# Attention groups in pairs on TensorE, turned context and 8-bit q, k, v

## The reference

```
def _fq(x, delta, zp, n_bits):
    xi = round(x / delta) + zp
    return (clip(xi, 0, 2**n_bits - 1) - zp) * delta
def _attn(x, ctx, wq, wk, wv, wo, bo, dq, dk, dv, dw):
    q, k, v = heads(x @ wq), heads(ctx @ wk), heads(ctx @ wv)      # 16 heads of 32
    sim  = _fq(q, dq, 128, 8) @ _fq(k, dk, 128, 8).T * SCALE
    attn = softmax(sim)
    out  = _fq(attn, dw, 0, 8) @ _fq(v, dv, 128, 8)
    return out @ wo + bo
h1 = _ln(x, ln1_g, ln1_b)
x = _attn(h1, h1, a1_wq, a1_wk, a1_wv, a1_wo, a1_bo, ...) + x
h2 = _ln(x, ln2_g, ln2_b)
x = _attn(h2, context, a2_wq, a2_wk, a2_wv, a2_wo, a2_bo, ...) + x
# then: layer norm, gated feed forward, residual; then block L1
```

## Time and profile before

| | us |
|---|---|
| median of 3 runs (2874.74 to 2876.45) | 2874.8 |
| the profiled execution | 2874.01 |
| its span, first to last instruction | 2872.2 |
| TensorE busy | 2700.3 (94%) |
| VectorE busy | 1690.5 (59%) |
| ScalarE busy | 1454.0 (51%) |
| GpSimd busy | 688.8 (24%) |

### The profile page before, as it was taken

The page is one execution under the profiler, slowest core; times in us unless marked ns, Lnnn a source line. Parts: engine busy times, 40 slices in busy tenths (PEclk is TensorE's granted clock), DMA queues, the critical chain, the costliest instruction groups (busy, mean ns, idle before and its releaser), DMA issues.

```text
span 2872.2 us, 54738 instructions
## 1 busy us (share of the span) xinstructions
PE 2700.3 (94%) x18432; PEld 2199.8 (77%) x18432; DVE 1690.5 (59%) x4154; ACT 1454.0 (51%) x3765; POOL 688.8 (24%) x1147
## 2 busy tenths in 40 slices
PE   5799999999999997589999999999999999999997
PEld 4566666666666665289999999999888888888885
DVE  6788888888888886453434343435434434434433
ACT  5577777777777775321111111113455555555554
POOL 1222222222222221132323232322212212212211
PEclk9899999999999998699999999999999999999998
DMA  5343333434334432441111111124111111111111
GB/s 151 85 85 83 83 82 84 84 83 88 84 80 86 91 77 59 107 135 66 66 66 66 67 64 73 58 80 155 38 44 48 55 44 44 58 44 44 58 37 37
DMA packets 337322, 211.07 MB, mean 73 GB/s; under 512 B 275568, under 2 KB 291952, under 8 KB 337264
## 3 DMA queue, kind: packets, MB, share of 16 engines
q1 hardware_dynamic: 337264, 210.34, 27.1%
HBM read 92.84 MB, written 50.33 MB: 50 GB/s over the span
## 4 chain that ended last, share of the span: by engine, by line
PE 54%; DVE 2%; issue 1%; ACT 1%; DMA 0%; POOL 0%; DVEq 0%; SPq 0%; POOLq 0%
PE AG L158 33%; PE Y L158 12%; PE XT L1287 2%; PE O L1310 2%; PE XT L1297 2%; PE XT L133 1%; DVE parts L1631 1%; DVE xhat L125 1%; PE Y L133 0%; PE O L1320 0%; DVE turned L187 0%; ACT stage L1527 0%; DMA stage<-in_ff_w_dram 0%; DVE mid_parts L1688 0%; POOL base L1841 0%
## 5 line engine op out<-in xcount | busy, mean ns | idle before, releaser
L158 PE MATMUL AG<-h_parts,up 128*128 128x256 f32 x6144 | 778.9, 285 | 13.4 <-DVE down L1612 10.1
L158 PEld LDWEIGHTS AG<-h_parts,up 128*128 128x128 f32 x6144 | 762.9, 193 | 25.9 <-issue 10.9
L594 ACT ACTIVATE e<-S,bias,qk_scale 128x256 f32<-128x256 f32 x1024 | 563.1, 563 | 66.7 <-DVE pq L707 62.9
L1495 ACT ACTIVATE gate<-AG,cols_pack 128x256 f32<-128x256 f32 x256 | 121.5, 474 | 671.3 <-PE AG L158 670.8
L1856 POOL TENSOR_TENSOR mid_parts<-mid_act,mid_parts 128x256 fp32r<-128x256 f32 x256 | 199.6, 780 | 1078.3 <-DVE mid_parts L1688 1078.3
L689 DVE TENSOR_REDUCE negmax<-S 128x4 f32<-128x1024 f32 x256 | 312.3, 1220 | 170.2 <-PE S L502 169.5
L158 PE MATMUL Y<-down,mid_parts 128*128 128x512 f32 x1536 | 403.8, 400 | 0.0
L1681 DVE SCALAR_TENSOR_TENSOR mid_act<-AG,cols_pack,gate 128x256 f32<-128x256 f32 x256 | 123.3, 482 | 423.9 <-ACT gate L1495 423.0
L158 PEld LDWEIGHTS Y<-down,mid_parts 128*128 128x128 f32 x1536 | 272.1, 189 | 68.5 <-issue 22.6
L707 DVE TENSOR_SCALAR pq<-e,rsum 128x256 uint16<-128x256 f32 x1024 | 291.9, 348 | 5.0
L564 ACT ACTIVATE shifted<-PJ,round_col,inv 128x512 f32<-128x512 f32 x192 | 149.2, 777 | 209.6 <-PE PJ L158 208.7
(11 more groups left out here) (131 smaller groups left out, 3707.0 us busy)
## 6 DMA issues: line engine op xcount, KB each, us to landing
stage<-in_ff_w_dram SPq DMA_DIRECT2D x48, 256.0 KB, 4.6
x_in<-in_x_dram SPq DMA_DIRECT2D x16, 512.0 KB, 3.7
ctx_in<-in_ctx_dram SPq DMA_DIRECT2D x16, 512.0 KB, 3.7
mid_dram<-x SPq DMA_DIRECT2D x16, 512.0 KB, 2.8
own<-mid_dram SPq DMA_DIRECT2D x16, 512.0 KB, 3.3
own<-in_ctx_dram SPq DMA_DIRECT2D x16, 512.0 KB, 3.5
h_dram<-h3T SPq DMA_DIRECT2D x16, 512.0 KB, 2.7
k_dram<-own SPq DMA_DIRECT2D x16, 512.0 KB, 2.6
```

Source lines behind the costliest of these rows:

```text
L158: last = nc.tensor.matmul(acc, lhs(l), rhs(r), start=(start and i == 0), stop=(stop and i == 2))
L594: nc.scalar.activation(e[:, s, i, :], S[s][:, i // 2, i % 2, :], ACT.Exp, bias=bias[:, s, i:i + 1], scale=qk_scale[:, ph.a:ph.a + 1], accu ...
L1495: nc.scalar.activation(gate[:, f % 2, :], AG[f % 2][:, TOK:2 * TOK], ACT.Gelu, bias=ff_b1[:, c:c + 1]).then_inc(gate_done, 1)
```

## The change

- Groups run through TensorE in pairs. At each odd g the scores of groups g + 1 and g + 2 are computed together: for each query tile four heads, one behind the other, on rows 0, 32, 64, 96, in four banks. They use both S tiles and wait for the exponentials of all groups up to g. Behind them come the products of the pair g - 5, g - 4, again four heads side by side for each half of the keys. pT has 4 buffers for 2.
- ctx arrives from the host in a turned layout; its transposes and the copies out of PSUM go, the casts and subtractions of high and low parts stay and are placed by group (`ctx_at`).
- ScalarE writes q, k, v as 8-bit integers (scaled copy, rounding and clipping in the conversion); VectorE only widens them to 16 bits, two groups after the fill where the clip was one group after.
- The order on the engines: ScalarE quantises and turns after a group's exponentials instead of before; VectorE computes quotients first and then, at odd g, both maxima; oT is copied at groups 0 and 4 of the next phase. k2's second fill moves ahead of q2, h2T from group 0 to 1, statistics of x from group 3 to 4.

The diff, cut to its core:

```diff
-                        4: [("ctxT", 0), ("ctxT", 1), ("o1", 0)], 5: [("o1", 1)], 6: [("v1", 0)], 7: [("v1", 1)]}
-        PHASE1_FILLS = {0: [("h2T", 0), ("h2T", 1), ("k2", 0)], 1: [("q2", 0)], 2: [("q2", 1)], 3: [("k2", 1)],
+                        4: [("o1", 0)], 5: [("o1", 1)], 6: [("v1", 0)], 7: [("v1", 1)]}
+        PHASE1_FILLS = {0: [("k2", 0)], 1: [("h2T", 0), ("h2T", 1), ("k2", 1)], 2: [("q2", 0)], 3: [("q2", 1)],
...
+            q8 = sb(one, "q8", [P, 2, D], I8)
+            pT = sb(one, "pT", [P, PAIR_BUFS, 4 * TT, P], F16)
...
             def pe_scores(pe, ph, g):
-                    pe.wait_ge(exp_done, 4 * (ph.group(g) - 1))
+                    pe.wait_ge(exp_done, 4 * ph.group(g))
+                for qt in range(TT):
+                    for i in range(4):
+                        r = DH0 * i
+                        ins = nc.tensor.matmul(S[i // 2][:, i % 2, qt, :],
+                                               qT[ph.tiles][r:r + DH0, g // 2, qt * P:(qt + 1) * P],
+                                               kT[ph.tiles][r:r + DH0, g // 2, :], start=True, stop=True)
...
             def pe_pv(pe, ph, g):
+                for kc in range(TT):
+                    for i in range(4):
+                        h = 2 * g + i
+                        r = DH0 * i
+                        c = 4 * (i % 2) + kc
                         ins = nc.tensor.matmul(O[half][r:r + DH0, (h // 4) % 2, :],
                                                vQ[ph.tiles][:, kc, h * DH0:(h + 1) * DH0],
+                                               pT[:, (g + i // 2) % PAIR_BUFS, c:c + 3:2, :], start=(kc == 0),
...
             def pe_phase(pe, ph, prev, nxt):
                 for g in range(GROUPS):
+                    if g % 2:
+                        if g + 1 < GROUPS:
+                            pe_scores(pe, ph, g + 1)
+                        elif nxt:
+                            pe_scores(pe, nxt, 0)
+                        if g >= 5:
+                            pe_pv(pe, ph, g - 5)
+                        elif prev:
+                            pe_pv(pe, prev, g + GROUPS - 5)
+                    for name, j in ph.steps(g):
+                        pe_fill(pe, at(ph.stage, ph.b, name, j))
...
-                nc.scalar.activation(shifted[:, bank, :], PJ[bank][:], ACT.Identity, bias=round_col[:, 0:1],
+                nc.scalar.activation(q8[:, bank, :], PJ[bank][:], ACT.Copy,
                                      scale=inv[:, d:d + 1]).then_inc(pj_emptied[bank], 1)
...
             def act_phase(act, ph, prev):
+                    if prev and g in (0, 4):
+                        act_oT(act, prev, g // 4)
+                    act_exp(act, ph, g)
+                    for where in late(ph, prev, g):
+                        if kind_of(where[2]) in QUANTISED:
+                            act_quantise(act, where)
+                    for where in transposed(ph, g, 0):
+                        act_transposed(act, where)
+                    if g == ph.ctx_at:
+                        act_ctx_high(act, ph, prev)
...
+            def dve_widen(dve, where):
+                wait_emptied(dve, where)
+                nc.vector.tensor_copy(dst, q8[:, bank, :]).then_inc(quantised, 1)
...
             def dve_phase(dve, ph, prev, nxt):
+                    fills = [f for f in late(ph, prev, g, 2) if kind_of(f[2]) in QUANTISED]
+                    if g:
+                        dve_probs(dve, ph, g - 1, fills)
+                    elif prev:
+                        dve_probs(dve, prev, GROUPS - 1, fills)
+                    into, m = (ph, g + 1) if g + 1 < GROUPS else (nxt, 0)
+                    if g % 2 and into:
+                        dve_max(dve, into, m)
+                    for where in transposed(ph, g, 1):
+                        dve_transposed(dve, where)
+                    if g % 2 and into:
+                        dve_max(dve, into, m + 1)
+                    if g == ph.ctx_at:
+                        dve_ctx(dve, ph, prev)
...
             def pool_phase(pool, ph, nxt):
+                    if g % 2:
+                        pool_dsum(pool, ph, g)
                      if g + 1 < GROUPS:
                         pool_bias(pool, ph, g + 1)
...
-                    pool_dsum(pool, ph, g)
+                    if g % 2 == 0:
+                        pool_dsum(pool, ph, g)
...
-                        sp.dma_start_transpose(pT[:, g % 2], pq[:, g % 2].rearrange("p j n -> p (j n)")).then_inc(
+                        sp.dma_start_transpose(pT[:, g % PAIR_BUFS],
...
-                        sp.dma_start(ctx_in[:], ctx_v[seq]).then_inc(ctx_loaded, 16)
+                        sp.dma_start(ctx_in[:], t["ctxT"][seq]).then_inc(ctx_loaded, 16)
```

More of the change, by code:

```diff
@@ L229, in build @@
         ROUNDS = B - 3
+        PAIR_BUFS = 4
         def bank_of(stage, name, j):
-            return 1 - j if name == "q2" else j
+            return 1 - j if name == "q2" and stage == "last" else j
         def fills_of(stage, bank):
@@ L272, in __init__ @@
                 self.tiles = a if tiles is None else tiles
+                self.ctx_at = {id(PHASE2_FILLS): 4, id(P_A_FILLS): 4, id(P_Y_FILLS): 0}.get(id(fills))
+                self.ctx_seq = 0 if stage == "first" else b + 1
                 self.early = ("o1", 1) in fills.get(3, [])
@@ L305, in turned_before @@
                 n += len(those("peeled"))
[L306 to L309, removed]
+            return n + len(those(stage, ORDER[stage][:ORDER[stage].index((name, j))]))
         WEIGHTS = ("a1_wq", "a1_wk", "a1_wv", "a2_wk", "a2_wq", "a2_wv")
@@ L342, in build @@
             x_in = sb(one, "x_in", [P, TT, D])
-            ctx_in = sb(one, "ctx_in", [P, TT, D])
+            ctx_in = sb(one, "ctx_in", [P, KC, TOK])
             x_bo = sb(one, "x_bo", [P, TT, D])
@@ L462, in pe_fill @@
                     ins = transpose_chunks(PJ[bank], xhat, j)
-                elif kind == "ctxT":
-                    seq = 0 if stage == "first" else b + 1
-                    pe.wait_ge(ctx_loaded, 16 * (seq + 1))
-                    ins = transpose_chunks(PJ[bank], ctx_in, j)
                 elif kind in ("o1", "o2"):
@@ L483, in pe_fill @@
                     from_ctx = kind in ("k2", "v2")
-                    pe.wait_ge(turned_low_done, 2 * turned_before(*where, ("ctxT",) if from_ctx else ("hT", "h2T")))
+                    if from_ctx:
+                        pe.wait_ge(ctx_low_done, 2 * (1 if stage == "first" else b + 2))
+                    else:
+                        pe.wait_ge(turned_low_done, 2 * turned_before(*where))
                     w = "a" + kind[1] + "_w" + kind[0]
@@ L604, in act_oT, with late @@
                                      scale=wv_scale[:, ph.a:ph.a + 1]).then_inc(oT_done, 1)
-            def late(ph, prev, g):
-                p, s = (ph, g - 1) if g else (prev, GROUPS - 1)
+            def late(ph, prev, g, by=1):
+                p, s = (ph, g - by) if g >= by else (prev, g + GROUPS - by)
                 if p is None:
                     return []
-                return [at(p.stage, p.b, n, j) for n, j in p.steps(s) if kind_of(n) not in ("hT", "h2T", "ctxT")]
+                return [at(p.stage, p.b, n, j) for n, j in p.steps(s) if kind_of(n) not in ("hT", "h2T")]
             def transposed(ph, g, j):
                 return [at(ph.stage, ph.b, n, i) for n, i in ph.steps(g)
-                        if kind_of(n) in ("hT", "h2T", "ctxT") and i == j]
+                        if kind_of(n) in ("hT", "h2T") and i == j]
             def act_phase(act, ph, prev):
@@ L708, in dve_probs @@
                                             ALU.mult, ALU.min).then_inc(prob_scaled, 1)
-                for where in fills:
-                    dve_unshift(dve, where)
             def dve_residual(dve, where):
@@ L779, in dve_drain @@
                 dve_probs(dve, ph, GROUPS - 1)
-                for where in late(None, ph, 0):
-                    dve_quantise(dve, where)
             def pool_bias(pool, ph, g):
```

224 lines of the change are left out of this document (83 added, 141 removed).

## The result

The changed kernel takes 2835.2 us (median; 2833.2 to 2836.7), the one before 2874.8 on the same chip: ratio 0.986, interval 0.984 to 0.987. It is faster by 39.6 us, less than half of the 87 forecast. The profiled execution has a span of 2834.9 us (before 2872.2). Its page: busy time by engine, and the granted clock of TensorE in 40 slices, in tenths.

A forecast was written before the change was run, and what follows sets the result against it. TensorE's own work was taken to bound the loop, then a chain a pair. 13 rounds from 68.5 to 64.0 us give -58.5, with the ends -87.3: 2788 us forecast, range 2762 to 2850.

The forecast's parts named there:

- Part 4: Cost of pairing in the attention loop: a chain closes once a pair; eight cycles between score bursts sum to 62.9 us.
- cycle 2/7: Phase 2, pair started by odd group 7 (v1, k2): 7.8 us, xhat between max and quotients delaying the second group.
- The clock term: Loop: one drop of TensorE's clock allowed a round, 1.1 us after the spare 0.4, making the round 64.0.
- Cycle 1/5: Phase 1, pair started by odd group 5 (o2, v2): 7.6 us between score bursts, with residual and xhat.
- 2/1: Phase 2, pair started by odd group 1 (q1, k1): 6.9 us between score bursts, set by the exponentials' chain.
- 2/3: Phase 2, pair started by odd group 3 (k1, o1): 7.5 us, the cast of ctx adding 0.55 on ScalarE.
- 1/3: Phase 1, pair started by odd group 3 (q2, o2): 7.1 us between score bursts, set by TensorE.
- second rival: Loop: dearer hand-overs, two or three clock drops a round or widening at 0.69; round 65.5 to 67.5, 2807 to 2835; chance 0.20.
- Part 1: Scores and products, four heads side by side: eight matmuls in 0.22 us where two groups took 0.65, saving 6.9 a round.
- Parts 2 and 3: Turned ctx saves 1.2 us of TensorE; 8-bit q, k, v: ScalarE's pass 0.6, conversion 0.34 in pitch, VectorE saves 2 a round.
- Ends: Attention stage outside the 13 rounds: start -7.5 us, peeled round -4.9, tail to the last o2 -16.4.

The follow-up runs named there:

- both repairs: Changed kernel with both x_bo additions moved to group 1 and the turned tile's low-part subtraction halved between VectorE and GpSimd: 2798.1 us, ratio 0.973.

## Why the prediction was wrong in size and right in kind

The direction, the new bound (a chain a pair, at 86 to 91% of TensorE), which cycles are the long ones and four of the eight lengths within 0.11 us came out as forecast. The gain was less than half. By the prediction's own steps:

- **Part 4, "GpSimd's 1.27 us additions fall before dsum of the odd group with 0.5 us or more to spare": failed.** I asked only whether GpSimd would be free for dsum, not what its addition does to VectorE beside it. x_bo waits for xhat, and before, what came behind xhat on VectorE was a max, from S in PSUM (the kernel before, VectorE and then GpSimd):

```profile
648.83 1.00 DVE L125 TENSOR_SCALAR xhat<-x,mv,rstd 128x512 f32<-128x512 f32 x2
649.74 1.22 DVE L689 TENSOR_REDUCE negmax<-S 128x4 f32<-128x1024 f32 x1
...
649.99 1.27 POOL L800 TENSOR_TENSOR x_bo<-x_in,rows 128x512 f32<-128x512 f32 x1 [1.03 <-DVE xhat L125]
```

  There the max lasts its usual 1.22. In pairs both max come first, so what stands behind xhat is a quotient, from e in SBUF, and the first one lasts 1386 to 1396 ns instead of 340, in each of the 13 rounds. Whether the place of the input or the kind of instruction makes the difference no run separates. Cost: 1.05 us a round in cycle 2/7, shown by moving x_bo, 13.7 us in all. The Trainium skill ("SBUF — State Buffer", SBUF: two separate sides) says that GpSimd and some instructions of VectorE (those in a 2-port mode or with two SBUF inputs) share one pair of ports, and that whichever starts first holds it for its whole instruction while the other waits. The quotient that starts 0.14 us after x_bo and ends 0.15 us after it agrees, and the sentence would have pointed at this step.
- **The clock term: 1.1 us a round forecast, 1.13 measured (66.53 - 65.40), but for another reason than I gave.** It is not the new transposing cycles by themselves: with x_bo moved, or the pause filled, 12 and 13 of 13 rounds keep the full clock. In this kernel it took the 2.65 us pause ahead of the transposes, which was 1.62 without x_bo in it. That the sizes agree is luck: I allowed a drop of 1.1 us in each round, and there were 7 in 13 rounds, four of 2.0 us, two of 1.8 and one of 3.1. x_bo's place cost some 24 us in all, as the run with it moved shows. The page of the Trainium skill that the prediction calls "the same" in its paragraph on the clock is "TensorE: Matmul & The Clock Gate".
- **Part 4, the other terms of the cycles: mis-sized by 0.06 to 0.35.** Cycle 2/7 without x_bo is 8.15 instead of 7.8: residual and statistics delay its max by more than the 0.4 that I took (1.06 after the scores, not 0.74). Cycle 1/5 is 7.95 instead of 7.6, and there the max is on time (0.43 after the scores at 655.03); it is the residual and xhat between max and quotients that hold back the second group's exponentials, to 5.6 after the scores where the sum had 5.3 (VectorE in the changed kernel):

```profile
655.46 2.36 DVE L676 TENSOR_REDUCE negmax<-S 128x4 f32<-128x1024 f32 x2 [0.47 <-PE S L501]
...
658.33 0.99 DVE L125 TENSOR_SCALAR xhat<-x_in,mv,rstd 128x512 f32<-128x512 f32 x2
...
659.45 1.14 DVE L694 TENSOR_SCALAR pq<-e,rsum 128x256 uint16<-128x256 f32 x4
```

  Moving xhat took back 0.36 and 0.81. The rest (2/1, 2/3 and four more) is 0.75 a round. In the cycles bound by the chain it is hand-overs: in 2/1 the max starts 0.43 after the scores, not 0.34, the first exponentials 2.05 after them, not 1.9, and the next scores come 0.19 behind ScalarE's second group, not 0.1; ScalarE's wait for the max, said to be 1.2, is 1.53 (607.23). In 1/3, where TensorE ends last, the packs took 0.22 more and the fills 0.19 less than forecast. In all 1.45 a round, 19 us. By its round (66.5, where it said 65.5 to 67.5) the result is the second rival, dearer hand-overs, which had a chance of 0.20; by its time (2835, where it said 2807 to 2835, and 67.5 a round with the ends of the forecast gives 2833) it lies at the edge of it, because of the ends. But neither cause that this rival named came: there were 7 drops in 13 rounds, not two or three in each, and the widening lasts 0.40, not 0.69.
- **Part 1: the mechanism failed, and it cost little.** Four heads do run side by side. But a pack of eight takes 0.32 and not 0.22: the 0.32 of four was never three slots, it was two waves and 0.10 us for the change of tile shape. A pair saves 0.64 us of TensorE instead of 0.86. Since the chain ends last in six of the eight cycles, this shows mainly as the first 0.1 of those. Its half-clock figures were no independent proof: 0.54 for four fits 3 x 0.18, but the single starts at 1145.31 are again two waves (0.17 apart), with the products 0.37 after the second. In the kernel with scores twice the sixteen at 650.71, at half clock, come in waves 0.19 to 0.21 apart, with the products 0.36 after the last: some 0.21 for a wave and 0.15 for the change. For eight at half clock the changed kernel shows 0.55.
- **Parts 2 and 3: right.** q takes 0.69 (0.57 in pitch, 609.41 to 609.98; forecast 0.6), the widening 0.40 long and 0.31 in pitch (607.97 to 608.28; forecast 0.34). Together with the turned ctx they are worth 24 us, more than half of the whole gain.
- **Ends: 15.6 us of the miss.** The first pairs are 0.9 us late from the start, and at the start and in the tail nearly every cycle is longer: in the tail 9.05, 11.45, 15.25, 7.17, 6.81, 11.23 and 16.8 to the last o2, forecast 7.5, 11.3, 12.8, 6.9, 6.4, 9.3, 15.3. The granted clock is 0.84 from 44 to 138 us and 0.81 in the tail, from 1040 to 1144. It was no better in the kernel before (0.84 from 44 to 139, 0.80 from 1070 to 1182). So a step that failed is the subtraction: the 95.9 and 85.9 us that I took away from held stretches at half clock, while I laid the new cycles from rows at full clock. How much of the 15.6 is the clock and how much waits no run here separates: this stays open.

Sum of the miss: 13.7 (x_bo) + 19.2 (the other terms) + 0 (clock) + 15.6 (ends) = 48.5 us.

## What to carry to other kernels

When a step is pushed later on one engine, ask what runs beside it on the engine that shares its way to memory, not only whether its own engine is free: here a 1.3 us addition off the critical path cost 24 us, and moving one line of GpSimd's order gave them back. A pause of TensorE can be paid for twice, if the clock falls with it; here both shortening and filling it helped. A stretch of before that held slow clock is not compared with a sum laid at full clock. And before overlap of small packs is counted, the pack's cost is to be split into waves and the change of tile shape, since only the first shrinks; the single starts in the trace show the waves.

## What the runs showed of the hardware

- VectorE's quotient (128x256, fp32 to 16 bits) beside a GpSimd addition of 128x512 that started 0.14 us ahead: 1386 ns instead of 340, ending 0.15 us after the addition. VectorE's max beside the same addition: its usual 1.22.
- GpSimd's subtraction of 128x512 (two SBUF inputs) that started 0.04 us behind VectorE's of the same size: 1.80 us instead of 1.26; VectorE's kept its 0.69.
- Score matmuls (tiles of 32 rows, 256 columns): 0.11 us a wave, as many heads at a time as there are strips of 32 rows, in any order of issue; 0.10 us on top once at the change to tiles of 32 columns. Eight, or four, take 0.32; sixteen of four heads 0.54; eight of two heads 0.55. At half clock some 0.21 a wave and 0.15 for the change.
- After a 2.65 us pause ahead of the transposes TensorE ran the next fill at half clock (5.40 us instead of 3.13) in 7 of 13 rounds; after 1.62 us in 1 of 13 (in none of 13 with both repairs); after 0.50 us in none. The pause alone doesn't settle it: with about the same 2.6 us it was 6 of 13 (heads one by one) and 9 of 13 (subtraction halved), with 2.48 us and scores twice every round had a cycle at half clock, and with single groups and waits of 1.05 and 0.50 us it was 6 of 13. What decides in a given round no run here shows.
